# Attention and FFN kernel: the product with v issued once per key tile at 512 columns instead of in two halves of 256

## What is computed

```
qkv = x @ w_qkv + b_qkv ;  q, k, v = 16 heads of 16 features each ; q, k = rope(q), rope(k)
attn = softmax(q @ k.T / 4)          # per sequence and head, 2048 x 2048
out  = attn @ v ;  x1 = layernorm(x + out @ w_out + b_out)
h    = silu(x1 @ w_gate.T) * (x1 @ w_up.T)   # weights are int8 values times 1/127, hidden 768
y    = layernorm(x1 + h @ w_down.T)
```

## Time and profile before

| | us |
|---|---|
| median of 3 runs | 2811.01 (2810.65 to 2816.54) |
| profiled execution, its own time | 2811.28 |
| its span, first to last instruction | 2809.5 |
| PE busy | 2778.3 (99%) |
| DVE busy | 2623.2 (93%) |
| ACT busy | 2568.9 (91%) |
| POOL busy | 1609.3 (57%) |

### The profile page before, as it was taken

How to read it: one execution, slowest core, us unless ns; L and a number is a source line. 1 busy time by engine, 2 the same in 40 slices (tenths; PEclk the granted TensorE clock), 3 DMA queues, 4 the chain that set the end, 5 groups by cost and what they waited for, 6 DMA issues and landing times. The chain is left out here.

```text
span 2809.5 us, 71055 instructions
## 1 busy us (share of the span) xinstructions
PE 2778.3 (99%) x27022; PEld 873.9 (31%) x27022; DVE 2623.2 (93%) x3423; ACT 2568.9 (91%) x5083; POOL 1609.3 (57%) x3888
## 2 busy tenths in 40 slices
PE   8998999999999999999999999999999999999998
PEld 5442222222222222222222222222222222256665
DVE  6879999999999999999999999999999999847777
ACT  6558999999999999999999999999999999875655
POOL 7673555555555555555555555555555555445653
PEclk9999999999999999999999999999999999999999
DMA  6422111111111111111111111111111111233431
GB/s 199 134 81 82 36 36 36 36 36 36 36 36 36 36 36 36 36 36 36 36 36 35 37 36 35 36 35 36 35 35 37 36 36 36 69 93 102 109 98 39
DMA packets 121381, 146.60 MB, mean 52 GB/s; under 512 B 52688, under 2 KB 87376, under 8 KB 121036
## 3 DMA queue, kind: packets, MB, share of 16 engines
q1 hardware_dynamic: 120892, 142.02, 17.8%
q10 hardware_dynamic: 144, 0.00, 0.0%
HBM read 106.30 MB, written 35.13 MB: 50 GB/s over the span
## 5 line engine op out<-in xcount | busy, mean ns | idle before, releaser
L1156 ACT ACTIVATE probs<-bank_ps 128x512 f32<-128x512 f32 x4096 | 2161.3, 614 | 22.9 <-PE bank_ps L1052 17.5
L112 DVE TENSOR_REDUCE tile_max<-s_ps 128x1 f32<-128x1024 f32 x1577 | 1819.5, 1215 | 1.0 <-PE s_ps L101 0.9
L1062 PE MATMUL bank_ps<-probs,kept_v 128*17 128x256 f32 x16384 | 1283.2, 385 | 0.0
L1052 PE MATMUL bank_ps<-q,k 64*128 64x512 f16 x4096 | 1243.1, 382 | 1.2 <-ACT probs L1156 0.8
L101 PE MATMUL s_ps<-k,q 64*128 64x512 f16 x4016 | 1218.9, 382 | 7.8 <-DVE tile_max L112 6.4
L131 POOL TENSOR_TENSOR larger<-spared 128x512 f32<-128x512 f32 x861 | 393.0, 456 | 651.3 <-ACT spared L1131 593.5
L1052 PEld LDWEIGHTS bank_ps<-q,k 64*128 64x128 f16 x4096 | 278.1, 93 | 905.0 <-ACT probs L1156 853.8
L1062 PEld LDWEIGHTS bank_ps<-probs,kept_v 128*17 128x17 f32 x16384 | 271.8, 95 | 788.7 <-issue 549.5
L135 POOL TENSOR_TENSOR spared<-spared,larger 128x512 f32<-128x512 f32 x861 | 391.9, 455 | 71.7
L133 POOL TENSOR_SCALAR larger<-larger 128x512 f32<-128x512 f32 x861 | 252.5, 293 | 75.3
L1185 DVE TENSOR_REDUCE tile_max<-s_ps 128x1 f32<-128x512 f32 x431 | 291.9, 677 | 0.8 <-PE s_ps L101 0.8
(11 more groups left out here) (128 smaller groups left out, 1815.1 us busy)
## 6 DMA issues: line engine op xcount, KB each, us to landing
q<-q_parts SPq DMA_DIRECT2D x193, 128.0 KB
k<-k_parts SPq DMA_DIRECT2D x193, 128.0 KB
x_t<-in_x_t SPq DMA_DIRECT2D x16, 512.0 KB, 8.6
q_parts<-parts SPq DMA_DIRECT2D x32, 256.0 KB, 3.1
k_parts<-parts SPq DMA_DIRECT2D x32, 256.0 KB, 3.1
heads_out<-sums SPq DMA_DIRECT2D x256, 32.0 KB, 2.1
kept_v<-heads_out SPq DMA_DIRECT2D x16, 512.0 KB, 5.6
kept_v<-inverses_out SPq DMA_DIRECT2D x32, 256.0 KB
```

The lines of the kernel that those rows point to most:

```text
L112: dve.tensor_reduce(s["tile_max"][h % 2][:, r // KW, r % KW:r % KW + 1], score_place(s, g)[:, columns], AX.X, ALU.max).then_inc(s["s_read" ...
L1052: pe.matmul(st_ps[n][:, :], k[h % 2][rows, kt * P:(kt + 1) * P], q[h % 2][rows, c * BANK:(c + 1) * BANK], start=True, stop=True).then_inc( ...
L1062: mm = pe.matmul(o_ps[h][c * 32:c * 32 + VM, at:at + HALF], t["kept"][:, h, kt, :], probs[(h * KT + kt) % RING][:, c * BANK + at:c * BANK ...
L1156: act.activation(probs[(h * KT + kt) % RING][:, c * BANK:(c + 1) * BANK], st_ps[n][:, :], ACT.Exp, scale=scale).then_inc(exp_done, 1)
```

## The change

A key tile's product with v is issued whole: four products of 512 columns, one per column group, in slots 3, 5, 7, ... (and slot 1 for the last key tile of the head before), in place of four products of 256 columns in every slot. The wait for the exponentials of the key tile stands at the same slot as before. After the loop one product is left instead of three halves. Nothing else changes: banks, rings, the other engines' programs. PE has half as many product instructions with v (8192 of 17-column weight loads and as many matmul passes in place of 16384), with the same number of columns in all.

```diff
@@ -1052,18 +1051,15 @@
-            def times_v(h, kt, half):
-
-                if half == 0:
-                    handed = kt == 0 and h > 0
-                    pe.wait_ge(exp_done, h * EXPS + (HANDED + 1 if handed else (kt + 1) * QC))
-                at = half * HALF
+            def times_v(h, kt):
+
+                handed = kt == 0 and h > 0
+                pe.wait_ge(exp_done, h * EXPS + (HANDED + 1 if handed else (kt + 1) * QC))
                 for c in range(QC):
-                    mm = pe.matmul(o_ps[h][c * 32:c * 32 + VM, at:at + HALF], t["kept"][:, h, kt, :],
-                                   probs[(h * KT + kt) % RING][:, c * BANK + at:c * BANK + at + HALF],
-                                   start=(kt, half) == (0, 0), stop=(kt, half) == (KT - 1, 1), tile_position=(0, c * 32))
-                if half == 1:
-                    mm.then_inc(pv_done, 1)
+                    mm = pe.matmul(o_ps[h][c * 32:c * 32 + VM, :], t["kept"][:, h, kt, :],
+                                   probs[(h * KT + kt) % RING][:, c * BANK:(c + 1) * BANK],
+                                   start=kt == 0, stop=kt == KT - 1, tile_position=(0, c * 32))
+                mm.then_inc(pv_done, 1)
@@ -1102,17 +1098,16 @@
                     before, half = divmod(n - 3, 2)
-                    if before >= 0:
-                        times_v(h, before, half)
-                    elif h > 0:
-                        times_v(h - 1, KT + before, half)
+                    if half == 0 and before >= 0:
+                        times_v(h, before)
+                    elif half == 0 and h > 0:
+                        times_v(h - 1, KT + before)
@@
-            for kt, half in ((KT - 2, 1), (KT - 1, 0), (KT - 1, 1)):
-                times_v(HEADS - 1, kt, half)
+            times_v(HEADS - 1, KT - 1)
```

More of the change, by code:

```diff
@@ L877, in attend @@
     EXPS = KT * QC
-    HALF = BANK // 2
     WIDE = 2 * BANK
```

## The result

The changed kernel takes 3003.6 us (median; 3002.4 to 3005.1), against 2812.7 for the kernel before, measured alongside: 1.068 times as long, 95% interval 1.066 to 1.070. The forecast was 2995 us. The profiled execution took 3004.7 us, 193.4 more than that of before; 184 were forecast.

The account below looks back on a forecast made before the run. PE was taken to bound the kernel before; the change makes a 2.37 us loop the bound. 61 regular heads at +2.89 us give +176; with the other heads and the end, +184, so 2995 us, range 2965 to 3040.

Parts of the forecast that it names:

- PE as the bound of the kernel before: Steady attention: PE issues back to back, 35.0 of 35.22 us a head, 0.2 to 0.4 over DVE.
- the first rival: The loop stays hidden and PE's saving counts until DVE bounds at 34.8 us a head: 26 us less, 2785 us; 4%.
- The saving on PE: PE's work in two slots shrinks from 2.19 to 1.99 us, mostly at changes between score pairs and products with v.
- The loop: From a through its exponential, d and the product with v to a′: 2.37 us per two slots, against 2.20 now.
- a: First of four transposed score products after a product with v; its exponential starts 0.42 us later and lasts 0.60.
- d: Fourth score product after a product with v; waits for a's exponential since three banks rotate; 0.31 us to the next product.
- a′: First score product after the next product with v, queued behind it on PE; starts 0.99 us after that product.
- What comes later than the loop: Check of the other engines: nothing exceeds 2.37 us; ACT idles 0.37 per cycle, DVE needs 2.26 for two full tiles.
- The product beside c: PE's first-pass product beside the third score product slips some 0.25 us waiting for DVE's buffer, and costs nothing.
- second rival: The loop lands between 2.17 and 2.26 us, so DVE's full tiles give 36.4 per head: +73, 2890 us; 4%.
- Once per head: The product with v of key tile 0 waits for a later exponential: 0.19 us more per head.
- third rival: DVE's buffer slip reaches the next turn's d, or PE's clock falls; a cycle of 2.47 gives 3095 us; 8%.

Follow-up runs that it names:

- run 10: Kernel before, with DVE's maximum of a full first-pass tile taken over 512 of its 1024 columns; 2808.8 us (0.9987).
- run 6: Changed kernel, with 256 in place of 512 columns in the product with v of key tiles 1 to 15 of each head; 2810.0 us.
- run 1: Changed kernel, with each product with v issued as two halves of 256 columns, one right behind the other in the same slot; 3011.5 us.
- run 2: Changed kernel, with 448 in place of 512 columns in the product with v of key tiles 1 to 15 of each head; 2914.7 us.
- run 4: Changed kernel, with the fourth exponential of each key tile taken over 256 of 512 columns; 2891.3 us.
- run 5: Changed kernel, with the fourth exponential of each key tile over 256 columns and DVE's maximum of a full first-pass tile over 512; 2793.3 us.
- run 3: Changed kernel, with DVE's maximum of a full first-pass tile taken over 512 of its 1024 columns; 3007.7 us.
- run 7: Kernel before, with the second half of each product with v moved ahead by one pair of score products; 3201.1 us (1.138).

## Why the prediction was right, point by point

- **PE as the bound of the kernel before, DVE close behind**: it holds. Run 10, with DVE relieved, gains 0.06 a head and no more. But DVE is closer, 0.17 us a head and not 0.2 to 0.4 (run 6). PE's 35.0 was too low as well (run 10: 35.16): the earlier trace rows don't show the one slot of a head that takes 1.24 us, from 1000.71 to 1001.95 in the kernel before, where PE waits for the exponential behind the sums' copy (the wait at 1001.07 in the earlier trace rows), and 31 × 1.094 + 1.24 = 35.15. With both the gain of the first rival was mis-sized: at best 8 to 10 us, where 26 were forecast.
- **The saving on PE (0.2 us in two slots)**: holds in PE's rows, though none of it reaches the time. Eight passes of 512 columns last 0.98 until the next pair, by the float32 passes of the earlier trace rows 0.99.
- **The loop, 2.37 us**: measured 2.38, with a → exponential 0.43, exponential → d 0.65, d → product with v 0.32, → a′ 0.98. Runs 1, 2, 4 and 5 show that the place of the work, its columns and ACT's latency count, and run 3 that DVE's buffer doesn't.
- **What comes later than the loop**: nothing, as said. The product beside c slips by 0.27; ACT idles 0.32 per turn (forecast 0.37) and 0.04 behind a spared copy, DVE 24.1 us in 600, that is 0.10 per turn. What I had not seen is the chain through both DVE and the product with v, 2.27 in the mean. I had DVE's own 2.26 in its place (second rival), and that its number 16 × 2.26 + 0.19 = 36.4 is that of run 4 is in part luck: DVE's own pace, spared tiles included, is 35.05 a head (run 6), and the chain makes the 36.43.
- **Once per head**: 38.25 − 16 × 2.38 = 0.17, forecast 0.19.
- **The sum**: 61 heads at +3.03 give +184.7 (forecast 176, from 2.89): the cycle's 0.01 is worth 10 us, as the bounds said. The first head gives +1.2 (forecast 2), the last but one +1.6 (1.5), the last and the end +4.9 (4.3), and 1.1 arises ahead of the attention, where nothing was changed or forecast. Together 193.4, read from one profiled execution of each kernel.
- **Clock**: no fall (granted clock 1.00 over 1000 to 1600 us and over the last head, 2638 to 2681), though PE now idles part of each turn. In runs 2 and 6, where PE has fewer columns, it did fall in the last head (0.68 over 2560 to 2580 us, 0.82 over 2443 to 2484), and in run 2 that head took 5 us longer than in the changed kernel. So this part of the third rival was a real one, though it didn't come about here.

## What to carry to other kernels

When work is moved into fewer, larger pieces on an in-order engine, go round every ring of buffers that crosses it: add up consumer latency, wake-up and all that the engine issues between the product that waits for a buffer and the next one its consumer waits for, and compare with the present pace. Total work and busy shares show none of this. Equal spacing may be what keeps several rings open at once. Here, with three PSUM banks towards ScalarE, a fourth score product between two lumps puts the whole lump into a loop, which sets the pace with 512 columns (2.38 us beside 2.19) and is hidden with 256 (run 6); with two tiles towards VectorE, a lump between the halves of a tile does the same (2.61, run 7). And before saving on the bounding engine, measure how far the next one is behind, by taking work off the first (here it was 0.4 to 0.5%).

## What the runs showed of the hardware

- A product with v whose 17 columns of weights go to each of four column groups streams float32 at the rate of a full-array product: 256 more columns cost (0.98 − 0.56) / 2 = 0.21 us per pass, beside 0.215 in the earlier trace rows. Two instructions of 256 columns in place of one of 512 cost 0.01 us per product more (run 1: 38.35 a head beside 38.25).
- A move of every second half of the product with v by a single pair of score products cost 388 us in run 7, twice what the change under study costs, with the same instructions on every engine.
- PE's granted clock was 1.00 over the last head of the changed kernel and fell to 0.68 (2560 to 2580 us) in that of run 2, which differs by 64 of 512 columns in the product with v. One execution of each was profiled; what decides between the two isn't shown.
